# Ten 512-column MLP and expert products as three fp32r passes, with the activations parted on GpSimd and the weights parted once

## The reference

```
o0 = gelu(xf @ e0_up.T) @ e0_down.T
o1 = silu(xf @ e1_w1.T) * (xf @ e1_w2.T) @ e1_down.T
o2 = gelu(gelu(gelu(xf @ e2_l1.T) @ e2_l2.T) @ e2_l3.T) @ e2_l4.T
o3 = gelu(gelu(xf @ e3_down.T) @ e3_up.T) @ e3_out.T
```

## Time and profile before

| what | us |
|---|---|
| median of 3 runs (881.12, 884.93, 885.28) | 884.93 |
| the profiled execution's own time | 880.93 |
| its span, first to last instruction | 879.1 |
| busy: TensorE, weight loads | 792.5, 482.2 |
| busy: VectorE, ScalarE, GpSimd | 635.8, 499.8, 299.6 |

### The profile page before, as it was taken

The page is one execution under the profiler, slowest core; times in us unless marked ns, Lnnn a source line. Parts: engine busy times, 40 slices in busy tenths (PEclk is TensorE's granted clock), DMA queues, the critical chain, the costliest instruction groups (busy, mean ns, idle before and its releaser), DMA issues.

```text
span 879.1 us, 18108 instructions
## 1 busy us (share of the span) xinstructions
PE 792.5 (90%) x5472; PEld 482.2 (55%) x5472; DVE 635.8 (72%) x1491; ACT 499.8 (57%) x960; POOL 299.6 (34%) x568
## 2 busy tenths in 40 slices
PE   3689999999899999989999998999999998999997
PEld 1554564745547555655647455475555555474555
DVE  1676479785888758886697858887588966978434
ACT  2325774467743785457744677436854576546652
POOL 4324514054331615136150443316151261504500
PEclk9998999999999999999999999999999999999999
DMA  4000000000000100000000000001000000000000
GB/s 162 1 8 14 14 1 1 9 15 25 0 1 8 36 0 0 7 12 25 0 0 7 13 24 0 1 7 37 1 0 7 12 26 0 0 7 13 24 1 13
DMA packets 15145, 11.73 MB, mean 13 GB/s; under 512 B 1040, under 2 KB 13968, under 8 KB 14992
## 3 DMA queue, kind: packets, MB, share of 16 engines
q1 hardware_dynamic: 15120, 11.43, 4.3%
HBM read 7.76 MB, written 2.10 MB: 11 GB/s over the span
## 4 chain that ended last, share of the span: by engine, by line
PE 55%; DVE 17%; ACT 14%; issue 12%; POOL 1%; ACTq 1%; DVEq 0%; POOLq 0%
PE R L443 38%; PE S L443 13%; DVE sb_mx L1194 7%; ACT sb_pr L1097 5%; DVE sb_x L1440 2%; ACT sb_es L1132 2%; PE S L448 1%; DVE sb_tokqk L1377 1%; ACT L961 1%; ACT sb_junk L1007 1%; ACT sb_yT L943 1%; DVE sb_kT L1400 1%; DVE sb_tokqk L1383 1%; PE R L448 1%; ACT sb_junk L1111 1%
## 5 line engine op out<-in xcount | busy, mean ns | idle before, releaser
L1097 ACT ACTIVATE sb_pr<-S 128x768 f32<-128x768 f32 (+1 forms) x192 | 165.9, 891 | 133.8 <-PE S L443 133.8
L1194 DVE TENSOR_REDUCE sb_mx<-S 128x2 f32<-128x256 f32 (+3 forms) x256 | 197.9, 817 | 32.3 <-PE S L443 30.2
L1708 POOL TENSOR_SCALAR_AFFINE_SELECT sb_pr<-sb_pr 128x256 f32<-128x256 f32 (+1 forms) x192 | 99.1, 518 | 315.2 <-ACT sb_pr L1097 312.6
L443 PE MATMUL R<-sb_pr,sb_va 128*32 128x512 f32 (+3 forms) x1024 | 89.6, 445 | 0.1
L443 PEld LDWEIGHTS S<-sb_maskb,sb_identb 128*128 128x128 bf16 x384 | 27.3, 98 | 89.7 <-DVE sb_mx L1194 74.7
L443 PE MATMUL R<-sb_xfT,sb_W 128*128 128x512 f32 x144 | 73.1, 613 | 3.3 <-ACT sb_pr L961 3.3
L443 PE MATMUL R<-sb_W,sb_pr 128*128 128x96 f32 (+1 forms) x512 | 70.9, 279 | 0.0
L443 PE MATMUL S<-sb_maskb,sb_identb 128*128 128x128 bf16 (+1 forms) x384 | 48.8, 240 | 22.6 <-DVE sb_mx L1194 19.7
L443 PEld LDWEIGHTS R<-sb_W,sb_pr 128*128 128x128 f32 x512 | 62.8, 192 | 4.4 <-issue 3.6
L443 PE MATMUL S<-sb_qT,sb_kT 32*128 32x256 f32 (+3 forms) x512 | 56.3, 384 | 5.1 <-ACT sb_pr L1097 4.3
L1634 POOL TENSOR_SCALAR sb_cv<-sb_xc,sb_vec 128x512 f32<-128x512 f32 x8 | 6.2, 779 | 152.8 <-DVE sb_tokqk L1383 152.8
(11 more groups left out here) (214 smaller groups left out, 1728.4 us busy)
## 6 DMA issues: line engine op xcount, KB each, us to landing
sb_xin<-x SPq DMA_DIRECT2D x9, 256.0 KB, 2.8
sb_W<-weights SPq DMA_DIRECT2D x1, 2290.0 KB, 10.0
sb_qT<-sb_mT SPq DMA_DIRECT2D x128, 4.0 KB
sb_xres<-x SPq DMA_DIRECT2D x8, 256.0 KB, 2.8
out<-sb_xres SPq DMA_DIRECT2D x7, 256.0 KB, 2.3
sb_cT<-sb_xact SPq DMA_DIRECT2D x8, 128.0 KB, 2.3
sb_W<-weights SPq DMA_DIRECT2D x1, 514.0 KB, 4.8
sb_cst<-consts SPq DMA_DIRECT2D x1, 328.0 KB, 3.1
```

The source lines that it names most:

```text
L443: return pe.matmul(o, lhsT, rhs, start=start, stop=stop, skip_group_check=True)
L1097: act.activation(pr[:, e % 4, :, 0:n], S[pair_of_exp(e)][:, :, 0:n], ACT.Exp).then_inc(p_sb, 1)
L1194: o = dve.tensor_reduce(mx[:, n // P - 1, g, heads[0]:heads[1] + 1], found[:, :, at_col:at_col + n], AX.X, ALU.max, negate=True)
L1708: pool.affine_select(out=keep, in_=keep, compare_op=ALU.is_ge, fill=0.0, base=0, pattern=pattern, channel_multiplier=-1)\
```

## The change

Ten products (e2a, w1, e1a, e1b) are computed as three fp32r passes, hi x hi, hi x lo and lo x hi, that add up in the PSUM bank. Weights are parted into hi and lo once, on GpSimd, in the first round between its `stage_b` and `stage_a`. In every tail GpSimd parts xfT and x1T (a copy to fp32r, then a subtraction), after its wait for the low parts of q and k and ahead of the convolution. TensorE waits for the parts before each of the ten. To make room, xact now shares memory with cv, x1n with yc, x1T with aoT and xf with xa, and waits for the sharing are added on ScalarE, VectorE and GpSimd. (Left out below: the new semaphores and their first increments, and the argument with which the first `norms` skips its new wait.)

```diff
@@ -81,6 +81,13 @@
+
+SPLIT = {}
+SPLIT_TOTAL = 0
+for _name in ("e2a", "w1", "e1a", "e1b"):
+    SPLIT[_name] = SPLIT_TOTAL
+    SPLIT_TOTAL += W_COLS[_name][1] - W_COLS[_name][0]
@@ -168,7 +175,7 @@
         cm = sb("cm", [P, L])
-        xact = sb("xact", [P, 3, L])
+        xact = cv
         cT = sb("cT", [P, L])
@@ -192,15 +199,15 @@
         x1 = sb("x1", [P, T, D])
-        x1n = sb("x1n", [P, T, D])
-        x1T = sb("x1T", [P, L])
+        x1n = yc[:].rearrange("p k (t c) -> p (k t) c", c=D)
+        x1T = aoT
         st2 = sb("st2", [P, T, 6])
...
         r3 = sb("r3", [P, 3, T])
-        xf = sb("xf", [P, T, D])
+        xf = xa
         xfT = sb("xfT", [P, L])
@@ -216,6 +223,8 @@
         gs = sb("gs", [P, T, D])
+        wpart = sb("wpart", [P, 2, SPLIT_TOTAL], F32R)
+        xpart = sb("xpart", [P, 2, 2, L], F32R)
@@ -628,7 +639,7 @@
-            def ring_free(r, k):
+            def ring_free(r, k, head=True):
                 if k == 0:
@@ -640,7 +651,7 @@
                 elif k - 4 == 15:
-                    pe.wait_ge(mT_sb, at(mT_sb, r, 1))
+                    pe.wait_ge(mT_sb, at(mT_sb, r, 1 if head else 0))
                 elif k - 4 in (16, 17):
@@ -662,6 +673,16 @@
+
+            def up_in_parts(r, k, name, n, which, head=True):
+
+                ring_free(r, k, head)
+                pe.wait_ge(part_sb, at(part_sb, r, 2 * which + 2))
+                a = SPLIT[name] + n * P
+                hi, lo = xpart[:, which, 0], xpart[:, which, 1]
+                mm(R[k % 4][:, :], wpart[:, 0, a:a + P], hi, True, False)
+                mm(R[k % 4][:, :], wpart[:, 0, a:a + P], lo, False, False)
+                mm(R[k % 4][:, :], wpart[:, 1, a:a + P], hi, False, True).then_inc(up_ps, 1)
@@ -779,16 +800,15 @@
-                x_in = [xfT[:]]
-                if tail:
-                    up(r, 3, "e2a", 0, x_in)
+                if tail:
+                    up_in_parts(r, 3, "e2a", 0, 0)
                 m_group(0, 0)
                 if tail:
-                    up(r, 4, "e2a", 1, x_in)
-                    up(r, 5, "w1", 0, [x1T[:]])
+                    up_in_parts(r, 4, "e2a", 1, 0)
+                    up_in_parts(r, 5, "w1", 0, 1)
                 m_group(0, 1)
                 if tail:
-                    up(r, 6, "w1", 1, [x1T[:]])
+                    up_in_parts(r, 6, "w1", 1, 1)
                     up(r, 7, "e3b", 0, [h3a[:]], 3)
@@ -797,30 +817,28 @@
                     up(r, 10, "e2b", 1, [h2a[:, 0], h2a[:, 1]])
-                    up(r, 11, "w1", 2, [x1T[:]])
+                    up_in_parts(r, 11, "w1", 2, 1)
                 m_group(1, 1)
                 if tail:
-                    up(r, 12, "w1", 3, [x1T[:]])
+                    up_in_parts(r, 12, "w1", 3, 1)
                     up(r, 13, "e2c", 0, [h2b[:, 0], h2b[:, 1]], 11)
...
                     up(r, 14, "e2c", 1, [h2b[:, 0], h2b[:, 1]])
-                    up(r, 16, "e1a", 0, x_in)
+                    up_in_parts(r, 16, "e1a", 0, 0)
                 m_group(2, 0)
                 if tail:
-                    up(r, 17, "e1a", 1, x_in)
+                    up_in_parts(r, 17, "e1a", 1, 0)
                 if head:
...
                 if tail:
-                    up(r, 18, "e1b", 0, x_in)
+                    up_in_parts(r, 18, "e1b", 0, 0)
                 m_group(2, 1)
                 if tail:
-                    if head:
-                        ring_free(r, 19)
-                    else:
+                    if not head:
                         pe.wait_ge(act_up, at(act_up, r, 12))
-                    mm(R[19 % 4][:, :], w("e1b")[:, P:2 * P], xfT[:]).then_inc(up_ps, 1)
+                    up_in_parts(r, 19, "e1b", 1, 0, head)
                 m_group(2, 2)
@@ -901,6 +919,7 @@
             pe.wait_ge(wt_loaded, 16)
+            pe.wait_ge(split_set, 2 * len(SPLIT))
             with pe.Fori(0, B - 1) as r:
@@ -990,6 +1009,8 @@
                     act.wait_ge(aoT_ps, at(aoT_ps, r, 1))
+                    act.wait_ge(up_ps, at(up_ps, r, 0))
+                    act.wait_ge(part_sb, at(part_sb, r, 0))
                     act.activation(aoT[:], R[0][:, :], ACT.Copy).then_inc(aoT_sb, 1)
@@ -1025,6 +1046,7 @@
                     act.wait_ge(x1T_ps, at(x1T_ps, r, 1))
+                    act.wait_ge(wo_ps, at(wo_ps, r, 1))
                     act.activation(x1T[:], R[1][:, :], ACT.Identity, bias=vec[:, V_LN2B:V_LN2B + 1],
@@ -1037,7 +1059,8 @@
                         act.wait_ge(xc_sb, at(xc_sb, r, n + 1))
-                        act.wait_ge(conv_sb, at(conv_sb, r, 0))
+                        act.wait_ge(y_ps, at(y_ps, r, 0))
+                        act.wait_ge(c_moved, at(c_moved, r, 0))
                         act.activation(cv[:, n], xc[:, n, TAPS - 1:TAPS - 1 + L], ACT.Identity,
@@ -1223,10 +1246,12 @@
-            def norms(r):
+            def norms(r, after_xf=True):
...
                 dve.wait_ge(xaT_ps, at(xaT_ps, r, 0))
+                if after_xf:
+                    dve.wait_ge(xfT_ps, at(xfT_ps, r, 1))
                 for t in range(T):
@@ -1352,6 +1377,7 @@
                     dve.wait_ge(xfT_ps, at(xfT_ps, r, 0))
+                    dve.wait_ge(xaT_ps, at(xaT_ps, r, 0))
                     for t in range(T):
@@ -1495,6 +1521,7 @@
                 else:
+                    dve.wait_ge(x1T_ps, at(x1T_ps, r, 1))
                     tt(yc[:, 0, :].rearrange("p (h d) -> p h d", h=NH),
@@ -1621,14 +1648,33 @@
+            def parts(r, which, src):
+
+                hi, lo = xpart[:, which, 0], xpart[:, which, 1]
+                pool.tensor_copy(hi, src).then_inc(part_sb, 1)
+                pool.wait_ge(part_sb, at(part_sb, r, 2 * which + 1))
+                tt(lo, src, hi, ALU.subtract).then_inc(part_sb, 1)
+
...
                     pool.sem_inc(pool_passed, 1)
+                if tail:
+                    pool.wait_ge(up_ps, at(up_ps, r, 0))
+                    pool.sem_inc(pool_passed, 1)
+                    pool.wait_ge(xfT_sb, at(xfT_sb, r, 1))
+                    pool.sem_inc(pool_passed, 1)
+                    parts(r, 0, xfT[:])
+                    pool.wait_ge(x1T_sb, at(x1T_sb, r, 1))
+                    pool.sem_inc(pool_passed, 1)
+                    parts(r, 1, x1T[:])
+                if head:
                     pool.wait_ge(xc_sb, at(xc_sb, r, 3))
                     pool.sem_inc(pool_passed, 1)
-                    pool.wait_ge(conv_sb, at(conv_sb, r, 0))
+                    pool.wait_ge(y_ps, at(y_ps, r, 0))
+                    pool.sem_inc(pool_passed, 1)
+                    pool.wait_ge(c_moved, at(c_moved, r, 0))
                     pool.sem_inc(pool_passed, 1)
@@ -1743,6 +1789,13 @@
             stage_b(-1, False, True)
+            pool.wait_ge(wt_loaded, 16)
+            for k, name in enumerate(SPLIT):
+                a, b = W_COLS[name]
+                hi, lo = (wpart[:, n, SPLIT[name]:SPLIT[name] + b - a] for n in range(2))
+                pool.tensor_copy(hi, W[:, a:b]).then_inc(split_set, 1)
+                pool.wait_ge(split_set, 2 * k + 1)
+                tt(lo, W[:, a:b], hi, ALU.subtract).then_inc(split_set, 1)
             stage_a(-1, False)
...
                 stage_b(r, True, True)
```

6 lines of the change are left out of this document (4 added, 2 removed).

## The result

Six runs of each kernel, on the same chip: before 884.12 us (881.12 to 885.28), after 891.83 us (889.85 to 895.54), a ratio of 1.0095, 95% interval 1.0072 to 1.0118. The change makes the kernel slower by about 1%. The six runs of the kernel after follow their mean granted clock: the two at 0.991 took 890.07 and 889.85 us, the one at 0.983 took 895.54. The profiled execution after took 892.72 us with a span of 891.0 and a mean granted clock of 0.985; before 880.93, 879.1 and 0.993. The two spans are 11.9 us apart.

What follows compares the result with a forecast made beforehand. VectorE and the score latency bound the kernel, TensorE second. From the profiled 880.93 us: +8.6 loop rounds, -3.1 for two already stopped, -1.5 last round, +1.0 first, +0.3 waits give 886.2; 887 said, range 876 to 894.

Steps and rivals of the forecast that it cites:

- One product: On TensorE, three fp32r passes take about 0.65 us in place of 0.86 for two fp32 records, 0.21 us less.
- Loop gain from products: In a loop round the shorter products save 0 us (bounds 0 and -1.77), as score groups wait for VectorE's maxima anyway.
- (a): VectorE's second small operation at 437.64, start of a loop round, probably slips in before GpSimd's subtraction: -0.45 us, otherwise +0.6.
- rival 3: Subtraction gets the port before the small operation, q/k chain starts 0.6 us late, tap stopped too: 890, up to 894; chance 0.19.
- (b): VectorE's taps at 444.56 and 447.35 run against GpSimd's later convolution and wait for it: +0.15 us a loop round.
- (c): GpSimd's time steps start 2.1 us later, so bias addition and decay product fall on VectorE's tap and gate operations: +1.53 us.
- rival 1: The collision misses, bias addition and decay product lying under maxima: about -0.3 a round, 875.5 or 879 us; chance 0.20.
- microsecond that decides: Argument for the missed collision: a microsecond decides whether GpSimd's late operations lie under maxima, and a copy's bounds are as wide.
- First round: GpSimd's parting of the weights meets the last taps of VectorE in the first round: +1.0 us, bounds 0 and +3.
- Last round: No scores there, so nine products are 1.9 us shorter, partly lost to waits for ScalarE: -1.5 us, bounds 0 and -1.9.
- number 4: The fourth of TensorE's numbered products, said to wait for ScalarE in the loop (0.47 us) and still in the last round.
- Waits: Waits added on VectorE in the scan and elsewhere: +0.3 us, bounds 0 and +1.

Runs made afterwards that it cites:

- Narrow_before: Kernel before with GpSimd's two late operations put in order, the ten fp32 products cut to 408 columns plus a bf16 identity filler: 876.88 us, ratio 0.9861.
- half_before: Kernel before with GpSimd's two late operations put in order, the ten fp32 products cut to 256 columns plus two bf16 fillers: 880.45 us, ratio 1.0010.
- order_after_wait: Changed kernel with GpSimd's two late operations put in order and its parting held behind VectorE's two 128x16 operations: 880.44 us, ratio 1.0005.
- parts_but_fp32: Changed kernel with all parting kept but the ten products left in plain fp32: 897.78 us, ratio 1.0099 against the kernel before.
- share_only: Changed kernel with plain fp32 products and no parting, only the shared buffers and their waits: 885.77 us, ratio 0.9969 against the kernel before.
- passes_twice: Changed kernel with products 17, 18 and 19 computed twice in every loop round: 902.00 us, ratio 1.0157 against the kernel before.
- the first experiments: The first group of four variants timed beside the kernel before, which stood at 887.8 us there.
- order_before: Kernel before with GpSimd's decay factors and bias addition made to wait for VectorE's gate operations: 878.77 us, ratio 0.9983.
- passes_no_parting: Changed kernel without parting of activations or its waits, the fp32r passes reading constant parts: 888.54 us, ratio 1.0002 against the kernel before.
- best_after: Changed kernel with all mends: parting, decay product and bias addition held later, weights parted earlier, last parting later: 875.99 us, ratio 0.9853.
- order_before_wait: order_before with GpSimd's convolution also held until VectorE's two 128x16 time-step operations are done: 881.84 us, ratio 0.9920 against the kernel before.

## Why the prediction was right or wrong

The time (887.0 said, 891.83 measured) lay in the range of 876 to 894, but on the side given 0.27, slower: from the median before, +2 us were said and +7.7 measured; from the profiled execution, +5.3 and +11.8. Step by step:

**One product: 0.65 us said, 0.72 measured**, 0.24 a pass and not 0.2. The slope of the earlier trace rows, 0.2 us for 512 columns, is 0.04 short of a pass. The saving is 0.14 us a product.

**Loop gain from products: 0 said.** Nearly right in size, wrong in reason. Narrow_before gives 0.27 us a round for 1.1 us of work taken off TensorE, half_before 0.47 for 2.8. The step that failed is "the scores only lie ready longer": I read VectorE as running without a gap from 448.38 on. In that round the tap at 457.03 was stopped (1.20 for 0.74) by the decay product, and that stop filled what otherwise is a 0.40 us wait for TensorE. VectorE and TensorE were within half a microsecond of each other, so a stop on one hides a gain on the other.

**(a) The small operation at the start: -0.45 said, +0.46 measured** (5.51 for 5.05). The bound I gave as the other case (+0.6, rival 3) came true: the subtraction starts 0.06 us ahead of line 1420. A matter of 0.06 us taken as probable; order_after_wait, with the parting behind these operations, brought lo to group from 5.50 to 4.64.

**(b) The taps: +0.15 said.** They are free (0.74). But line 1336, the step-ratio operation next to the tap, takes 0.77 (0.6 too much). I had counted two-input operations only. Behind it the second reductions start 3.63 us after the first ones and not 3.24 (453.35 - 449.72, before 445.45 - 442.21), and of these 0.39 us some 0.15 come back by the ninth group: the measured +0.24 of the length. The Trainium skill ("SBUF — State Buffer", section "Who interferes with whom") has `tensor_scalar` among the operations that can take the shared pair when their operands meet its conditions; the trace agrees, down to 16 columns.

**(c) Bias addition and decay product on the gate operations: +1.53 said, about 0 measured** in six of seven rounds. The step that failed is "the time steps start 2.1 us later". They wait for line 1339 anyway, GpSimd had 3.39 us of idle time ahead of them, and the convolution ended at 455.33 against 455.32 for line 1339: no delay. This is half of rival 1, which had 0.20: the bias addition lies under the maxima, the decay product still stops the tap. The "microsecond that decides" is 0.01 us: whether a small GpSimd operation comes 0.03 or 0.04 us behind a tap. It went well in six rounds of this execution and ill in all seven of parts_but_fp32, so nothing in the diff could have told it; that the six went well is luck. The price was off too: the 1.53 us came from the first loop round, which is 0.1 to 0.3 us longer than its like in every kernel here; a stopped round is 1.35 us longer than its like.

**First round: +1.0 said, +1.44** in the length, of the same kind as foreseen (+2.2 in the period, 0.46 of it the clock's). **Last round: -1.5 said, +0.6** from where its products start. The nine products are shorter by 9 x 0.14 = 1.3, but three stopped gate operations make ScalarE's exponential late, and TensorE waits 1.83; I had the parting on TensorE's queue only, not on VectorE's there. That number 4 "still waits for ScalarE" in this round was wrong too: before, TensorE runs through (842.79, 4.61 us for ten records). **Waits: +0.3 said, 0** (share_only is not slower).

**Not foreseen: the clock**, +4.5 in loop rounds, and 1.6 at the start that are this execution's and not the change's. A fall of 3.4 us at the ninth group is paid with 1.5 us. That less work can bring it without any fp32r pass in the ten products is shown by half_before, at nearly twice the change's saving; that work put back takes the stretches away, by passes_twice. That less work is the whole cause in the kernel after is argued from these two and the order of the fourteen profiles, not shown: no run took off exactly as much. Nor need the kernel before be free of falls: beside the first experiments its 23 runs had mean clocks of 0.988 to 0.994, where its one profile has 0.993, and a fall of 3.4 us lowers that mean by about 0.002 (an estimate, half of 3.4 in 880). No profile shows where its clock fell in the runs at 0.988.

So the sum missed each of its larger terms, and they cancelled in part: +1.23 a round said, +0.70 and 0.6 of clock measured. That the number came out in the range is luck and a wide range. Right were that the columns saved are not the time saved, and that GpSimd's stops on VectorE decide.

**On the median:** that it was nearer to a kernel stopped in every round than the profiled execution fits: order_before, which has no such stop, took 878.8 us, and the unchanged kernel stood at 879.9 us beside it and at 887.8 and 889.3 on two other chips, on the first of which share_only and passes_no_parting were stopped seven times of seven; 878.8 + 7 x 1.35 = 888.3. The clock is not the whole of it: at mean clocks of 0.993 and 0.994 the unchanged kernel took 879.3 to 880.4 us beside order_before and 886.6 to 887.5 beside share_only; there, between 0.994 and 0.988, lie some 4 us more. No profile of the kernel before was taken there, so the stops are argued, not shown.

**Open:** what puts the clock down in one round and not in the next of the same kernel. Narrow_before idles 0.38 and 1.01 us and kept the full clock, best_after idles 0.47 and 1.03 and lost it in two rounds. TensorE has 94.8 us of work a round in the first and 94.2 in the second; whether these 0.6 us or the passes make the difference was not tested.

## What to carry to other kernels

Before moving work to GpSimd, list VectorE's operations of 0.2 us that will stand beside it: they cost up to the length of the GpSimd operation, and one semaphore wait that holds GpSimd until they are through gave more here (0.51 us a round) than shorter products did (0.27 and 0.47 in narrow_before and half_before). The same wait in the kernel before only moved the stop, so look where the GpSimd work lands next. Where two engines are within half a microsecond of each other, a shorter step on one moves the wait and little else; look for a stop that hides the second limit. Two variants can differ by 1% only in how one close pair of operations falls out (and perhaps two chips), so put that pair in order in both before judging a change.

## What the runs showed that was not expected

A one-input VectorE operation of 128x16 is stopped as well as a two-input one (0.77 us in the kernel after, 1.14 in order_before_wait, 0.17 free). An idle time of about 1 us in a round that is otherwise 90% busy was followed by 3.4 us of TensorE at 1.2 GHz in three of seven rounds (370.22: 1.03 us for the masks that take 0.61), and by 6.8 us once in passes_no_parting and once in half_before. And a small GpSimd operation goes ahead of a VectorE tap that starts 0.025 to 0.037 us before it and waits for one that starts 0.039 us or more before it, in every profile here, with 1.35 us of the round behind it.
